# A second product on TensorE for the first layer norm of a Mamba, attention and expert kernel

## The reference, cut to what matters

```python
x = mamba(x); x = silu(group_norm(x)) + x_in       # called x1 in the kernel
t = to_tokens(x)
t = t + attention(layernorm(t))                    # the first norm
t = t + experts(layernorm(t))                      # the second norm

def layernorm(x, eps=1e-05):
    m = mean(x, axis=-1); v = var(x, axis=-1)      # over the 64 channels of a token
    return (x - m) / sqrt(v + eps)
```

## Time and profile before

| | us |
|---|---|
| median of 3 runs | 1405.29 (1405.14 to 1409.21) |
| the profiled execution, its own time | 1405.26 |
| span of the profiled execution | 1403.4 |
| busy PE, DVE, ACT, POOL in the span | 1032.5, 1116.6, 684.2, 487.1 |

### The profile page before, as it was taken

How to read it: one execution, slowest core, us unless ns; L and a number is a source line. 1 busy time by engine, 2 the same in 40 slices (tenths; PEclk the granted TensorE clock), 3 DMA queues, 4 the chain that set the end, 5 groups by cost and what they waited for, 6 DMA issues and landing times.

```text
span 1403.4 us, 16864 instructions
## 1 busy us (share of the span) xinstructions
PE 1032.5 (74%) x6132; PEld 431.9 (31%) x6132; DVE 1116.6 (80%) x1398; ACT 684.2 (49%) x1178; POOL 487.1 (35%) x257
## 2 busy tenths in 40 slices
PE   3255325858886898779877998689868976986984
PEld 1001101323333333323333334233333333433442
DVE  5695359898899998999899989998999987258235
ACT  3324212438644774367446654576437702740660
POOL 3262336335442543353255334444425421000000
PEclk9557556979987999889987998899879997999895
DMA  2640583154425333534335433543154321120000
GB/s 45 165 120 31 124 169 82 40 143 123 100 64 141 97 80 90 134 91 110 72 96 125 117 82 81 123 115 81 51 135 104 81 58 41 35 50 1 2 16 8
DMA packets 40937, 120.25 MB, mean 86 GB/s; under 512 B 9222, under 2 KB 9610, under 8 KB 38475
## 3 DMA queue, kind: packets, MB, share of 16 engines
q1 hardware_dynamic: 27030, 68.83, 21.1%
q10 hardware_dynamic: 13824, 50.34, 14.4%
HBM read 95.65 MB, written 17.20 MB: 80 GB/s over the span
## 4 chain that ended last, share of the span: by engine, by line
DVE 39%; PE 28%; issue 9%; ACT 3%; POOL 2%; DMA 1%; DVEq 0%; ACTq 0%; SPq 0%
DVE row_max L979 16%; DVE state L1045 8%; PE ps L1436 6%; PE ps L1421 5%; DVE drive L1054 4%; PE ps L1304 3%; PE ps L1216 2%; PE ps L1196 2%; PE ps L1405 2%; ACT probs L866 2%; PE ps L1201 2%; DVE moe L1136 2%; PE ps L1207 1%; PE ps L1353 1%; PE ps L1424 1%
## 5 line engine op out<-in xcount | busy, mean ns | idle before, releaser
L711 POOL TENSOR_TENSOR read<-state,c_rep 128x1024 f32<-128x1024 f32 x128 | 311.3, 2434 | 365.5 <-DVE state L1045 271.9
L866 ACT ACTIVATE probs<-ps 128x512 f32<-128x512 f32 (+3 forms) x768 | 327.2, 499 | 109.2 <-PE ps L1424 79.1
L979 DVE TENSOR_REDUCE row_max<-ps 128x1 f32<-128x640 f32 (+7 forms) x352 | 328.8, 985 | 39.0 <-PE ps L1308 38.0
L1045 DVE TENSOR_TENSOR_SCAN state<-decay,drive 128x1024 f32<-128x1024 f32 x96 | 265.3, 2764 | 1.6 <-DVE drive L1054 1.2
L1421 PE MATMUL ps<-q_stack,k_stack 128*128 128x512 bf16 (+3 forms) x768 | 214.6, 345 | 65.4 <-DVE drive L1054 28.7
L1304 PE MATMUL ps<-k_stack,q_stack 128*128 128x512 bf16 (+3 forms) x704 | 200.0, 365 | 72.0 <-DVE row_max L979 70.0
L821 ACT ACTIVATE decay<-decay,a_scale 128x1024 f32<-128x1024 f32 x128 | 147.1, 1154 | 100.8 <-DMA decay<-dt_dram 100.8
L1353 PE MATMUL ps<-u_rows,pick 128*128 128x512 bf16 x256 | 113.1, 466 | 100.3 <-DVE state L1030 73.7
L1436 PE MATMUL ps<-probs,v_aug 128*32 128x512 f32 (+3 forms) x1536 | 168.2, 510 | 8.8 <-ACT probs L866 3.7
L1421 PEld LDWEIGHTS ps<-q_stack,k_stack 128*128 128x128 bf16 x768 | 75.9, 100 | 253.7 <-ACT probs L866 65.1
L1054 DVE TENSOR_TENSOR drive<-ps,b_rep 128x512 f32<-128x512 f32 x192 | 127.7, 678 | 21.0 <-PE ps L1353 19.3
(11 more groups left out here) (184 smaller groups left out, 1262.7 us busy)
## 6 DMA issues: line engine op xcount, KB each, us to landing
decay<-dt_dram ACTq DMA_DIRECT2D x96, 512.0 KB, 4.7
decay<-dt_dram SPq DMA_DIRECT2D x32, 512.0 KB, 6.1
q_stack<-q_parts_dram SPq DMA_DIRECT2D x48, 192.0 KB
k_stack<-k_parts_dram SPq DMA_DIRECT2D x48, 192.0 KB
u_rows<-read SPq DMA_DIRECT2D x96, 64.0 KB, 2.0
k_parts_dram<-read SPq DMA_DIRECT2D x40, 128.0 KB, 2.4
dt_dram<-read SPq DMA_DIRECT2D x8, 512.0 KB, 2.6
q_parts_dram<-read SPq DMA_DIRECT2D x24, 128.0 KB, 2.3
```

The costliest lines, as they stand in the source:

```text
L711: pool.tensor_tensor(read[:, k % (2 * NG), :], state[:, k % 2, :], c_rep[:, :], ALU.mult)\
L866: act.activation(probs[:, e % (2 * QUAD), 0:w], bank_of(("scores", e))[:, 0:w], ACT.Exp, scale=SCALE).then_inc(exped.sem, 1)
L979: dve.tensor_reduce(row_max[:, i, h0:h0 + nh], scores[:, :, 0:P * (i + 1)], AX.X, ALU.max, negate=True).then_inc(row_maxed.sem, 1)
L1045: dve.tensor_tensor_scan(state[:, k % 2, :], decay[:, k % DECAYS, :], drive[:, k % 3, :], 0.0, ALU.mult, ALU.add).then_inc(scanned.sem, NH)
```

## The change

The centred values of the first norm are no longer made by DVE. PE makes them with a second product: x1 as the stationary operand and `less_mean`, the 64 by 64 identity less 1/64 everywhere, as the moving one. It goes to bank 3, ahead of the eight transposes to bank 2, both before step 26. ACT squares bank 3 into `xn`, copies it to `xcen`, waits for the transposes and copies bank 2 to `t1`. DVE's `centre_first` goes. POOL waits for the copy `xcen` too before it scales. Three entries of the hand-written order move by one place each: the third `last_folds` from step 4 to 5, `group_mean_product` from step 13 to 12, the last scan unit from round 25 to 26. `conv_rows` is loaded into a part of `z_gate`, and POOL builds `less_mean` in the setup with two more instructions.

```diff
@@ -92,7 +92,6 @@
         w_z = sb("w_z", [P, DI])
-        conv_rows = sb("conv_rows", [P, 2 * DI])
         conv_bias = sb("conv_bias", [P, 1])
@@ -113,6 +112,7 @@
         ident_bf = sb("ident_bf", [P, P], BF16)
+        less_mean = sb("less_mean", [C, C])
         mask_q = sb("mask_q", [P, P], BF16)
@@ -182,6 +182,7 @@
         a_spread = z_gate[:, T // 2:T // 2 + P].rearrange("p (n e) -> p n e", e=CH)
+        conv_rows = z_gate[:, T - 2 * DI:T]
 
@@ -210,7 +211,7 @@
                 load(w_z[0:C, :], W_in[:, DI:2 * DI])
-                load(conv_rows[:, :], conv_w.rearrange("(a d) k -> a (d k)", a=1).to_broadcast([P, 2 * DI]))
+                load(conv_rows, conv_w.rearrange("(a d) k -> a (d k)", a=1).to_broadcast([P, 2 * DI]))
                 load(conv_bias[:, :], conv_b.rearrange("(d a) -> d a", a=1))
@@ -241,7 +242,7 @@
 
-                conv_k = conv_rows[:, :].rearrange("p (d k) -> p k d", k=2)
+                conv_k = conv_rows.rearrange("p (d k) -> p k d", k=2)
                 for rows, tap in ((slice(0, C), 1), (slice(C, 2 * C), 0)):
@@ -305,6 +306,8 @@
                 diagonal(ident[:, :], [[-1, P]], 0)
+                then(pool.memset(less_mean[:, :], -1.0 / C))
+                diagonal(less_mean[:, :], [[-1, C]], 0, 1.0 - 1.0 / C)
                 diagonal(ident_bf[:, :], [[-1, P]], 0)
@@ -340,7 +343,7 @@
 
-        UNITS_IN = (4, 0, 2, 1, 2, 0, 2, 0, 2, 1, 2, 2, 0, 1, 2, 0, 1, 0, 1, 1, 2, 1, 2, 1, 1, 1, 0, 0)
+        UNITS_IN = (4, 0, 2, 1, 2, 0, 2, 0, 2, 1, 2, 2, 0, 1, 2, 0, 1, 0, 1, 1, 2, 1, 2, 1, 1, 0, 1, 0)
         FOLDS = ((0, 0, 13), (0, 1, 8), (1, 0, 20), (1, 1, 20))
@@ -377,7 +380,7 @@
         gn_ps = signal("gn_ps", 1)
-        t1_ps = signal("t1_ps", 1)
+        t1_ps = signal("t1_ps", 2)
         xnt_ps = [signal("xnt_ps_1", NH), signal("xnt_ps_2", NH)]
@@ -421,7 +424,7 @@
         gn_gated = signal("gn_gated", 1)
-        ln_chain = [signal("ln_chain_1", 3), signal("ln_chain_2", 3)]
+        ln_chain = [signal("ln_chain_1", 1), signal("ln_chain_2", 3)]
         centred = [signal("centred_1", 1), signal("centred_2", 1)]
@@ -680,6 +683,7 @@
                         pool.wait_ge(ln_rstd[0].sem, ln_rstd[0].at(p, 1))
+                        pool.wait_ge(centred[0].sem, centred[0].at(p, 1))
                         scale(pool, 0, p)
@@ -759,7 +763,10 @@
                     def take_t1():
-                        square(0, p)
+                        act.wait_ge(t1_ps.sem, t1_ps.at(p, 1))
+                        act.activation(xn[:, 0, :, :], tokens_by_channels(3), ACT.Square).then_inc(squared[0].sem, 1)
+                        act.copy(xcen[:, 0, :, :], tokens_by_channels(3)).then_inc(centred[0].sem, 1)
+                        act.wait_ge(t1_ps.sem, t1_ps.at(p, 2))
                         if not p.is_first:
@@ -957,13 +964,9 @@
                            .then_inc(ln_chain[n].sem, 1)
-                        dve.wait_ge(ln_chain[n].sem, ln_chain[n].at(batch, 3))
+                        dve.wait_ge(ln_chain[n].sem, ln_chain[n].at(batch, ln_chain[n].per))
                         dve.tensor_scalar(ln_s[:, n, 3, :], ln_s[:, n, 2, :], 1.0 / C, LN_EPS, ALU.mult, ALU.add)\
                            .then_inc(ln_var[n].sem, 1)
-
-                    def centre_first():
-                        dve.wait_ge(t1_ps.sem, t1_ps.at(p, 1))
-                        centre(0, p, tokens_by_channels(2))
 
@@ -985,7 +988,7 @@
                         (18, c and not b, lambda: less_high(dve, c)), (18, c and not b, lambda: less_mid(dve, c)),
-                        (22, p, gate_group_norm), (26, p, centre_first), (28, p, lambda: variance(0, p)))
+                        (22, p, gate_group_norm), (28, p, lambda: variance(0, p)))
                     for s in range(NSCORE):
@@ -1243,6 +1246,10 @@
                         for i in range(TB):
+                            last = pe.matmul(banks(3)[:, i * C:(i + 1) * C], x1[:, tokens(i)], less_mean[:, :],
+                                             start=True, stop=True)
+                        last.then_inc(t1_ps.sem, 1)
+                        for i in range(TB):
                             last = pe.transpose(banks(2)[:, i * C:(i + 1) * C], x1[:, tokens(i)], ident[0:C, 0:C])
@@ -1311,8 +1318,8 @@
                     beside = (
-                        ((1, 1), c, convolution), ((0, 2, 4, 5), p, last_folds), ((6, 8), c, gate_projection),
-                        ((9, 11), p, out_projection), ((11, 12), c, dt_before_bias), ((13,), p, group_mean_product),
+                        ((1, 1), c, convolution), ((0, 2, 5, 5), p, last_folds), ((6, 8), c, gate_projection),
+                        ((9, 11), p, out_projection), ((11, 12), c, dt_before_bias), ((12,), p, group_mean_product),
                         ((14, 15), c, b_product), ((17, 20), c, c_product), ((24,), b, value_projection),
```

## The result

The changed kernel takes 1411.24 us (median of 15 runs, 1406.21 to 1417.72), the kernel before 1405.29 (15 runs, 1400.96 to 1412.31). The ratio is 1.0039, 95% interval 1.0021 to 1.0057: about 0.4% slower, where 1415 (0.7%) was forecast. The profiled execution of the changed kernel is one of the slower ones, 1416.13 us with a span of 1414.3, and is 10.9 us over the profiled one of the kernel before.

A forecast was written before the change was run, and what follows sets the result against it. DVE (39% of the chain) or PE (28%) sets the end, by place. Batches 10.7 + first batch 0.7 + setup 0.1 - scan unit 1.25 = 10.2 us on 1405.26, rounded down to 1415; range 1405 to 1421.

The forecast's parts named there:

- The mechanism: Step 26: product, transposes and scores follow x1 on PE; 3.06 us instead of 2.61 at full clock, 5.2 at half.
- rival 3: Step 26: product as short as the transposes, 0.61 us at full clock, 0.97 at half; 1401 or 1397; chance 0.10.
- The count of passes at half clock: Step 26, seven batches: four at half clock, two at 0.45 us, the last at 0.8; 10.7 us slower.
- PE may be back sooner: Step 26: busier PE may regain its clock, so a half-clock batch costs 2.25 us, between 1.9 and 2.6.
- Batch 0: First batch, no scores to hide anything: x1 to the square takes 3.5 us instead of 2.78, 0.7 slower.
- The setup: Setup: two more POOL instructions, 0.7 us, hidden to within 0.1; the `conv_rows` load costs 0.
- The moved unit: Last scan unit, round 25 to 26: its 0.68 us wait goes, mostly not passed on; 1.25 us gained.
- The group mean: Step 12: scores now stand behind the moved group mean; between 0 and 0.1 us a pass, taken as 0.
- ACT's copy: Copy to `xcen` after the product: about 0.57 us, hidden, no cost; without cover 4 us.
- Rival 1: Step 26: the product keeps PE at 2.4 GHz; +1.6 us, 1407; chance 0.20.
- Rival 2: Step 26: half clock at every batch; +17.8 us, 1423; chance 0.12.
- Rivals 3 and 4: Step 26: rival 3, and another that all DVE's centring time is gained, 14 us, 1391; the latter's chance 0.04.

The follow-up runs named there:

- run 3: Changed kernel with the product replaced by eight more transposes of x1, the mean not subtracted; 1398.06 us, ratio 0.9961 to the kernel before.
- run 2: Changed kernel with the three moved order entries back at their old places, so only the product is new; 1416.04 us, ratio 1.0079 to the kernel before.
- run 10: Changed kernel with ACT's copy to `xcen` done twice, POOL's scaling waiting for the second; 1411.33 us, ratio 1.0037 to the kernel before.
- run 1: Kernel before with only the three moved order entries, centring still on DVE; 1407.75 us, ratio 1.0017.
- run 11: Kernel before with only the last scan unit moved from round 25 to 26; 1404.75 us, ratio 1.0006.
- run 5: Kernel before with transposes and DVE's centring moved from step 26 to 28, variance from 28 to 30; 1426.64 us, ratio 1.0155.

## Why the prediction came true, point by point

**The mechanism** was right. Product, transposes and scores of step 26 follow each other on PE behind x1, and DVE idles meanwhile. DVE's wait is 2.75 us at full clock and 4.5 to 5.0 in the other six passes, a little over what was forecast. In the pass above, the product takes 3.35 us to the start of the transposes, these 0.99, the scores 0.86: 5.20, where 3.4, 0.97 and 0.8 had been put down. At full clock the whole is 2.93 instead of 3.06. The two instructions for each block, read off the attention projection, decided. A product as short as the transposes would have been faster (run 3: 5.5 us below before, rival 3 had said 4.3 to 8).

**The count of passes at half clock** was mis-sized for this execution: six instead of four, 15.7 us instead of 10.7. "PE may be back sooner" was true, but of the time after the product, not in it: that is the 4.5 us given back up to `max_parts`, a term that the sum lacked. The two misses nearly cancel: 11.2 us instead of 10.7, and 10.9 for the whole span instead of 10.2. That this sum comes so close is luck. It is also the sum of one slow execution: by the ratio, the change costs 5.5 us in the median run, about half of the forecast's 10.2. Other executions have another mix: with the full product and the transposes before step 26, the interval is 15.7 us longer than before in the changed kernel's trace, 11.2 in run 2's and 8.5 in run 10's. Runs without a profile have only their mean clock over the whole span on record. Over the 15 of the changed kernel it is 0.859 in the five slowest and 0.864 in the five fastest, and run 10's 1403.22 us had 0.869. This fits, but it does not say where the clock was lost, so that the median is 5 us below the profiled run because of this mix is argued, not shown.

**Batch 0:** predicted +0.7. The product starts at 146.69 and the square at 150.37,

```profile
146.69 3.64 PE L1249 MATMUL ps<-less_mean,read 64*128 64x64 f32 x16 [15.26 <-POOL read L681]
...
150.37 0.60 ACT L767 ACTIVATE xn<-ps 128x512 f32<-128x512 f32 x1 [8.62 <-PE ps L1249]
```

3.68 us instead of 2.78, so +0.9. The forecast had taken off the end of the last product, which overlaps what follows on PE; but here ACT waits for that end. The +1.0 of the whole stretch has two more parts. x1 comes 0.4 later, and DVE's scan work behind it 1.3 later (162.15 instead of 160.84); 0.3 of that is gone by `gate_scan`.

**The setup** was put at 0.1 and is part of that 0.4. PE's first convolution starts at 17.09 to 17.13 us in the nine traces with the changed setup and at 16.82 to 16.93 in the five without. So it costs about 0.25 us; which part of it does was not tried.

**The moved unit:** the wait of the convolution for the heads' division appears as predicted, in four passes:

```profile
531.24 1.52 PE L1199 MATMUL ps<-xs,w_conv 128*128 128x512 f32 x3 [0.46 <-DVE attn L1074]
```

Predicted was a gain of 1.25 us. The stretches that hold it are 1.4 and 1.6 us shorter in this trace, and run 1 has 1.65 and run 11 has 1.56 in the first of them. The times of run 11 put the move between 0.2% faster and 0.3% slower, so whether the predicted 1.25 us is there stays open.

**The group mean** was taken at 0 and costs 0.11 us a pass (0.7 in six), at the end of its bounds (run 1). The last pass has 1.0 more in the same stretch, where an output projection ran at half clock, 1.97 us instead of 1.07. Run 11, which has no product, shows 23.12 us in that stretch of its last pass instead of 21.46, so this comes without the change too.

**ACT's copy** was costed at nothing, and doubling it changed nothing (run 10).

**The rivals.** Rival 1 (the clock is given back during the product, 1407) failed: 0.50 to 0.55 in six of seven. The rule of the Trainium skill behind it (TensorE: Matmul & The Clock Gate, Part 1, that activity releases the throttle) agrees with the trace only behind the product, where the mean clock of the pass shown is 0.96 instead of 0.84. Rival 2 (all at half, 1423) was nearly met in its count, six of seven; what came back behind step 26 kept the sum at the forecast's. Rivals 3 and 4 were out: DVE's 14 us vanished from its busy time and came back as idle time.

## What to carry to other kernels

Before moving work off the engine with the largest share of the chain, look at what it would do instead and whether that is ready: here DVE's centring ran while PE caught up and hid PE's slow clock, and the same work on PE was exposed and paid at that clock. Take the cost of a new product from the nearest row of the same shape and type, at both clocks, and follow the clock behind it too. A step of a hand-written order has a due time that shows only when it is missed: two steps later for the centring made PE stand 3.1 us at `xn_to_channels`, and moved a short DVE instruction into POOL's work, where it took up to 1.95 us instead of 0.17. When one move lifts two waits, sort the passes before giving the gain to one of them.

## What the runs showed of the hardware that was not expected

The float32 product against a 64 by 64 operand is two instructions for each block, and each is also longer than a transpose. At full clock the 16 take 1.80 us from their start to the start of what follows (277.18 to 278.98), 0.11 each; the eight transposes take 0.59 (to 279.57), 0.07 each.

A DVE instruction on 8 elements of each partition took 0.17 us with POOL idle and 1.50 us in the pass of run 5 that is shown above, beside a POOL instruction that had started before it (first DVE, then POOL):

```profile
570.16 1.50 DVE L949 TENSOR_SCALAR ln_s<-ln_s 128x8 f32<-128x8 f32 x1
```

```profile
569.51 2.12 POOL L536 TENSOR_TENSOR read<-decay,read 128x1024 bf16<-128x1024 f32 x1 [1.16 <-ACT read L794]
```

It ends at 571.66, when POOL does (571.63). In the kernel before it was 0.53 at the same place. The 14 traces hold 376 such instructions (TENSOR_SCALAR, 128x8). All 251 that run beside no POOL instruction take 0.17 us. The other 125 run beside POOL's work on 128x1024, and none of them ends before it; in the 110 that take over 0.25 us, DVE ends 0.02 to 0.03 us after POOL. The longest takes 1.95 us, in run 5.

The Trainium skill has a rule on this: GPSIMD Engine Reference, section 1, Specifications, says that GpSimd shares its SBUF interfaces with VectorE, with contention for DVE instructions in a 2-port mode or with two SBUF inputs. The two ends that fall together agree with it; no run here varied the mode.
